# One graph-network kernel on one core: row statistics moved to ScalarE, narrower one-hot windows, merged VectorE instructions

## The chip, the core and the metric

The kernel runs on one core of one Trainium2 chip. A core has TensorE (PE, matrix products into PSUM), VectorE (DVE), ScalarE (ACT), GpSimd (POOL) and SyncE (SP, which here only issues DMAs). Each engine takes its own instructions in order and waits on semaphores for the others. The metric is the device time of one execution in microseconds (us); lower is better. Before the change it is 123.3 us, the median of three runs (123.14 to 123.56).

## The reference

The input is x, 625 nodes by 256 features, 10,625 edges (src, dst; sorted by dst) and one weight for each edge.

```
edge_conv(h, W, b):  m = concat(h[dst], h[src]-h[dst]) @ W + b;  s = segment_sum(m, dst);  return s / max(count, 1)
h = relu(layernorm(x));  xs = [h]
for W, b in three layers:  h = relu(edge_conv(h, W, b));  xs.append(h)
x = x + concat(xs) @ Wf + bf
h = relu(layernorm(x)) @ W4
agg = segment_sum(edge_weight * h[src], dst) + b4;  h = batchnorm over nodes (gamma, beta)
out = x + relu(h)
```

## The kernel before

Gathers and segment sums are done as products with two dense 625 x 625 matrices: `counts` (how many edges run from node s to node d) and the matrix of edge weights (`parts`, the weight split into three bf16 parts so that no accuracy is lost). They are built first, from about 4 to 49 us, and the three layers, the head and the last convolution follow as plain matrix products.

**The build.** The 10,625 edges are 85 tiles of 125 edges. For each tile t one engine makes `src_hot`, a one-hot row of all node numbers for each edge's source (125 x 628, bf16): VectorE with one comparison (`source_tile`, L537), or, for the tiles named in `SCALAR_TILES`, ScalarE with two activations (`distance`, then `src_hot`, L864 and L867). Before the change ScalarE makes tiles 0, 4, 9, 13 early and 38, 57, 76 later. As dst is sorted, a tile's destinations lie in a window of 28 nodes (`WINDOW`). `dst_hot` holds for each block of 17 tiles the one-hot window (`plain_window`, L525) and its products with the three weight parts (`weighted_window`, L531, three instructions). TensorE multiplies the two (L1168, `place`) and adds into five PSUM banks, one for each source block s, four kinds side by side. It goes through five destination blocks r; the list `window_pieces(r)` says which tiles touch block r and with how many nodes (19 or 21 pieces each), so block r costs 5 x 19 or 5 x 21 matmuls with 4 x width columns. For r = 0 the five banks advance tile by tile; for later r bank after bank. ScalarE copies each finished bank out (`copy_block`: `counts`, `parts`). `src_hot` is a ring of 36 tiles; tile t may be written when the blocks that read tile t-36 are done.

**Between the tiles.** Into VectorE's sequence of tiles other work is put at fixed tile numbers: the row statistics of x at tile 8 (`STATS_AT`, five L483 and five L489), reciprocal and shift at tile 11 (`SHIFT_AT`), the vectors and a ones matrix at 19, the low parts of the five neighbour terms u at `U_AT` (L549), the weight differences W_top - W_bottom at `DIFF_AT` (L544), the check of the window's fit at 40 and 74. ScalarE computes the square root (L852), then h0 = relu(norm(x)) in five rows (L898); TensorE transposes them between the pieces of block 0 (L1058), ScalarE copies them back (`h_t`), and after block 0 TensorE computes the neighbour terms of layer 0 (L1079, `neighbour_terms_0`), after block 1 the own terms (L1090). From tile 36 on VectorE also waits for blocks.

**After the build.** `sum_counts` (L1142) adds the counts over sources with a ones matrix, 5 matmuls for each of three column groups; VectorE takes reciprocals (`inverse_rows`, L608, L610) and has_edge (L615). GpSimd waits until all of VectorE's source tiles are made (L441), adds weight parts, splits one weight matrix (L435) and masks the own terms (L452). `sums_0` (L1243, L1264) multiplies u with counts, in two halves of columns; `z_step` (L694 scaling, L698 adding the masked own terms), ScalarE's h_hi (L963) and `h_low` (L704) give layer 1's input; TensorE meanwhile does `head_0` (L1100) and then `neighbour_terms(1)`, which waits for the first two h_low before block 0 and for all four before block 2. Each high part is a copy to a reduced-precision type on ScalarE, each low part the remainder on VectorE.

## Time and profile before

| | before |
|---|---|
| time, median of 3 runs | 123.3 us |
| the profiled execution's own time | 123.12 us |
| its span (first to last instruction) | 121.3 us |
| PE busy, share of the span | 105.4 us, 87% |
| DVE busy | 96.2 us, 79% |
| ACT busy | 59.3 us, 49% |
| POOL busy | 27.6 us, 23% |
| chain that ended last, by engine | PE 58%, DVE 30%, ACT 5%, DMA 2% |

The span starts with the first instruction; the 1.8 us between span and time lie outside it. A busy share is an average over stages; which engine sets the pace in a stage is read from the chain that ended last and from the waits. In the rows further down "start us, us" is the start from the span's begin and the duration. Durations of neighbours overlap a little, so the cost of one of many is the distance of two starts.

### The profile page before, as it was taken

The page shows a single profiled execution, that of the slowest core. Times are in us where ns is not written, and L with a number is a line of the kernel's source. Part 1 is how long each engine was busy: PE and PEld are TensorE (multiplying, and loading weights), DVE is VectorE, ACT ScalarE, POOL GpSimd, SP SyncE. Part 2 cuts the span into 40 slices and gives each one's busy share as a digit, 9 for nine tenths or more (in the row PEclk, how much of TensorE's full clock was granted, in tenths as well). Part 3 has the DMA queues.
Part 4 walks back from the last instruction along what each step waited for, and adds up shares of the span by engine and source line. Part 5 has one row for each costly group of instructions (what it writes and reads, how often), then busy time and mean ns, then how long its engine had stood idle before and what let it go on. Part 6 is the DMA issues. An engine that isn't in the chain of part 4 may idle for free.

```text
span 121.3 us, 2679 instructions
## 1 busy us (share of the span) xinstructions
PE 105.4 (87%) x1034; PEld 97.7 (81%) x1034; DVE 96.2 (79%) x273; ACT 59.3 (49%) x140; POOL 27.6 (23%) x38
## 2 busy tenths in 40 slices
PE   0395799979998899999999999999899997999740
PEld 0355588958797799999899999999799997998630
DVE  0699967999999998859996759966799979707970
ACT  2297988833979877602371313450703343313530
POOL 7100000000000019983329920089300000000000
PEclk9999999999999999999999999999999999999995
DMA  2979400000020002300000300000000000000025
GB/s 48 242 193 268 157 0 5 0 5 0 0 95 0 0 5 67 114 5 3 0 0 6 86 0 0 5 0 0 0 5 0 0 0 0 8 0 0 0 66 146
DMA packets 5402, 4.63 MB, mean 38 GB/s; under 512 B 556, under 2 KB 5387, under 8 KB 5387
## 3 DMA queue, kind: packets, MB, share of 16 engines
q1 hardware_dynamic: 4460, 3.68, 11.2%
q10 hardware_dynamic: 926, 0.75, 2.3%
q8 instruction: 10, 0.16, 0.6%
q14 instruction: 6, 0.04, 0.1%
HBM read 3.79 MB, written 0.64 MB: 37 GB/s over the span
## 4 chain that ended last, share of the span: by engine, by line
PE 58%; DVE 30%; ACT 5%; DMA 2%; issue 2%; SPq 0%
PE bank L1264 13%; DVE src_hot L537 12%; PE bank L1019 9%; PE bank L1021 9%; PE bank L1020 9%; PE bank L1168 8%; PE bank L1100 4%; DVE dst_hot L531 3%; DMA edge_rows_i<-in_dst_dram 2%; DVE stats L483 2%; PE bank L1304 2%; ACT h L898 2%; PE bank L1243 2%; DVE raw L544 1%; DVE u_lo L549 1%
## 5 line engine op out<-in xcount | busy, mean ns | idle before, releaser
L1168 PE MATMUL bank<-dst_hot,src_hot 125*128 125x112 bf16 (+4 forms) x505 | 27.0, 209 | 3.2 <-DVE src_hot L537 2.7
L1168 PEld LDWEIGHTS bank<-dst_hot,src_hot 125*128 125x128 bf16 x505 | 25.0, 99 | 5.8 <-DVE src_hot L537 4.3
L537 DVE TENSOR_SCALAR src_hot<-node_id,edge_cols 125x628 bf16<-125x628 f16 x78 | 24.3, 374 | 0.0
L441 POOL TENSOR_TENSOR parts<-parts 125x625 f32<-125x625 f32 x5 | 7.5, 1502 | 50.1 <-DVE src_hot L537 41.4
L1264 PE MATMUL bank<-counts,u_lo 125*128 125x312 f32 (+1 forms) x60 | 16.3, 307 | 0.0
L963 ACT ACTIVATE h_hi<-pre 128x312 fp32r<-128x312 f32 (+1 forms) x12 | 5.6, 466 | 18.4 <-DVE pre L698 18.4
L1264 PE MATMUL bank<-counts,u_hi 125*128 125x312 f32 (+1 forms) x48 | 14.0, 307 | 0.0
L842 ACT ACTIVATE parts<-bank 125x375 f32<-125x375 f32 x25 | 12.3, 493 | 0.0
L1264 PEld LDWEIGHTS bank<-counts,u_lo 125*128 125x128 f32 x60 | 10.9, 189 | 0.0
L842 ACT ACTIVATE counts<-bank 125x125 fp32r<-125x125 f32 x25 | 7.0, 281 | 6.0 <-PE bank L1168 5.8
L1264 PEld LDWEIGHTS bank<-counts,u_hi 125*128 125x128 f32 x48 | 9.1, 189 | 0.0
L549 DVE TENSOR_TENSOR u_lo<-bank,u_hi 125x256 fp32r<-125x256 f32 x15 | 6.1, 420 | 3.4 <-ACT u_hi L842 3.1
L1021 PE MATMUL bank<-wf_lo,h_hi 128*125 128x256 f32 x30 | 8.4, 281 | 0.0
L1019 PE MATMUL bank<-wf_hi,h_hi 128*125 128x256 f32 x30 | 8.4, 281 | 0.0
L1020 PE MATMUL bank<-wf_hi,h_lo 128*125 128x256 f32 x30 | 8.4, 281 | 0.0
L842 ACT ACTIVATE u_hi<-bank 125x256 fp32r<-125x256 f32 x15 | 5.7, 383 | 4.3 <-PE bank L1021 3.9
L694 DVE TENSOR_TENSOR pre<-bank,inv_count 128x312 f32<-128x312 f32 (+1 forms) x12 | 5.7, 477 | 2.4 <-PE bank L1264 2.4
L842 ACT ACTIVATE weights_hi<-bank 125x500 fp32r<-125x500 f32 (+1 forms) x7 | 3.4, 546 | 7.5 <-PE bank L1304 7.5
L698 DVE TENSOR_TENSOR pre<-pre,own 128x312 f32<-128x312 f32 (+1 forms) x12 | 6.3, 524 | 1.0 <-POOL own L452 0.6
L864 ACT ACTIVATE distance<-node_id,edge_cols 125x628 f16<-125x628 f16 x7 | 5.8, 825 | 2.3 <-DVE edge_cols L520 2.2
L1019 PE MATMUL bank<-weights_hi,u_hi 125*128 125x312 f32 (+1 forms) x20 | 6.2, 312 | 0.7 <-DVE u_lo L761 0.7
L704 DVE SCALAR_TENSOR_TENSOR h_lo<-pre,h_hi 128x312 fp32r<-128x312 f32 (+1 forms) x12 | 6.3, 534 | 0.7
...
## 6 DMA issues: line engine op xcount, KB each, us to landing
raw<-in_L_gnn_W_dram SPq DMA_DIRECT2D x3, 512.0 KB, 6.5
...
raw<-in_L_gnn_Wf_dram SPq DMA_DIRECT2D x1, 512.0 KB, 3.7
...
```

The lines of the kernel that those rows point to most:

```text
L441: step.add(pool.tensor_tensor(part[:, :, 1, :], part[:, :, 1, :], part[:, :, 2, :], ALU.add))
L537: dve.tensor_scalar(src_hot[:, t % RING, :], node_id[:, :], edge_cols[:, 0, t:t + 1], None, ALU.is_equal).then_inc(src_hot_vector, 1)
L549: dve.tensor_tensor(u_lo[:, b, :], groups.bank[name][0:BLK, 0:D], u_hi[:, b, :].bitcast(F32), ALU.subtract).then_inc(u_lo_ready, 1)
L698: dve.tensor_tensor(pre_t[:, f, a:e], pre_t[:, f, a:e], own[:, f, a:e], ALU.add).then_inc(z_ready, 1)
L704: dve.scalar_tensor_tensor(out=h_lo[l + 1][:, f, a:e], in0=pre_t[:, f, a:e], scalar=0.0, in1=h_hi[l + 1][:, f, a:e].bitcast(F32), op0=ALU.max,
L842: copy = lambda o, i: nc.scalar.activation(o, i, ACT.Copy)
L864: nc.scalar.activation(distance[:, :], node_id[:, :], ACT.Abs, bias=edge_cols[:, 0, t:t + 1], scale=-1.0).then_inc(distance_ready, 1)
L1019: pe.matmul(o, lh, rh, start=start, stop=False)
L1020: pe.matmul(o, ll, rh, start=False, stop=False)
L1021: return pe.matmul(o, lh, rl, start=False, stop=stop)
L1168: return pe.matmul(built[s][:, :, n0:n0 + n], src_hot[:, t % RING, BLK * s:BLK * s + P], dst_hot[:, c, :, j // 2, c0:c0 + n, j % 2], start ...
L1264: ins = pe.matmul(bank[KF * h + f][:, 0:e - a], u[:, k, P * f:P * (f + 1)], counts[:, k, a:e], start=False, stop=(k == NB - 1 and u is u_l ...
```

## The change

- The mean and variance of x move from VectorE (five statistics and five aggregations at tile 8) to ScalarE: five passes with Identity whose accumulator output gives the row sums, one small scaling, five passes with Square whose accumulator output gives the sums of squares, and the root. VectorE's shift is a product with the negative mean, at tile 12. ScalarE makes no early source tiles; it makes 36, 40, 55, 72 and 76.
- The three parts of the edge weight are copied by ScalarE, with VectorE doing the subtractions in between.
- The windows that TensorE reads are narrowed by `half_width(t)`: 12 nodes at the ends of the list, then 16, 20 and 24, and 28 in the middle. The number of matmuls stays at 505.
- The degree of a node is no longer summed from five blocks: a column of ones in `src_hot` (number 626) makes it an extra row of the last source block, and `sum_counts` reads that row with one matmul (two for the last column group).
- `weighted_window` is one instruction of 1512 elements in place of three of 504. The u terms of layer 0 are handled two blocks at a time. Source tiles are 626 wide.
- The differences of W1 and W2 move behind the tiles on VectorE; GpSimd waits for the first low part after them. The constants' memsets move from GpSimd to VectorE's idle start. In the batch norm at the end the semaphore's numbers go down by one with the removed aggregation.

```
+def half_width(t):
+    p = (t + 0.5) / TILES
+    return min(WINDOW // 2, 2 * round(2.5 + 9 * math.sqrt(p * (1 - p))))
...
-            pool.wait_ge(src_hot_vector, TILES - len(SCALAR_TILES))
+            pool.wait_ge(w_lo_vector, 1)
...
             def weighted_window(c):
                 dve.wait_ge(window_ready, c + 1)
-                for k in range(1, KINDS):
-                    part = weight_parts[:, k - 1, c, :].rearrange("p (a b) -> p a b", b=2)
-                    ins = dve.tensor_tensor(dst_hot[:, c, k], dst_hot[:, c, 0],
-                                            part.unsqueeze(2).to_broadcast([EP, PAIRS, WINDOW, 2]), ALU.mult)
-                ins.then_inc(weighted_windows_ready, 1)
+                shape = [EP, KINDS - 1, PAIRS, WINDOW, 2]
+                part = weight_parts[:, c].rearrange("p k (a b) -> p k a b", b=2).unsqueeze(3).to_broadcast(shape)
+                plain = dst_hot[:, c, 0].unsqueeze(1).to_broadcast(shape)
+                dve.tensor_tensor(dst_hot[:, c, 1:KINDS], plain, part, ALU.mult).then_inc(weighted_windows_ready, 1)
...
-                if t == STATS_AT:
-                    dve.wait_ge(x_loaded, 32)
-                    for b in range(NB):
-                        moments_of(b)
-                    variances(range(NB))
                 if t == SHIFT_AT:
-                    scale_shift(range(NB), norm_ready)
+                    stds[0] += 1
+                    dve.wait_ge(std_ready, stds[0])
+                    step.add(dve.reciprocal(rstd[0:BLK, 0:NB], rstd[0:BLK, 0:NB]))
+                    step.wait()
+                    dve.tensor_tensor(shift[0:BLK, 0:NB], neg_mean[:, :], rstd[0:BLK, 0:NB],
+                                      ALU.mult).then_inc(norm_ready, 1)
...
+            difference(1)
             low_part(HI_WB1, wb[1][1][:, :, :], raw[1][:, KF:2 * KF, :], wb[1][0][:, :, :])
-            low_part(HI_WD1, wd[1][1][:, :, :], raw[1][:, 0:KF, :], wd[1][0][:, :, :])
             inverse_rows(0)
+            low_part(HI_WD1, wd[1][1][:, :, :], raw[1][:, 0:KF, :], wd[1][0][:, :, :])
             inverse_rows(1)
...
             edge_rows_of(1)
+            difference(2)
...
-            act.wait_ge(edge_cols_ready, 1)
-            act.wait_ge(constants_ready, 4)
-            for t in SCALAR_EARLY[:3]:
-                source_tile(t)
...
+            act.wait_ge(x_loaded, 32)
+            act.wait_ge(padding_ready, 1)
+            for b in range(NB):
+                nc.scalar.activation(h0[:, b, :], x_in[:, b, :], ACT.Identity,
+                                     accum_out=row_sums[:, b:b + 1]).then_inc(row_sums_ready, 1)
+            act.wait_ge(row_sums_ready, NB)
+            nc.scalar.activation(neg_mean[:, :], row_sums[:, :], ACT.Copy, scale=-1.0 / D).then_inc(mean_ready, 1)
+            act.wait_ge(mean_ready, 1)
+            for b in range(NB):
+                nc.scalar.activation(h0[:, b, :], x_in[:, b, :], ACT.Square, bias=neg_mean[:, b:b + 1],
+                                     accum_out=row_squares[:, b:b + 1]).then_inc(row_squares_ready, 1)
...
-                for s in blocks:
-                    ins = pe.matmul(o[:, 0:e - a], ones_r[:, :], part[:, s, a:e], start=(s == 0 and part is counts),
-                                    stop=(s == NB - 1 and part is counts), skip_group_check=True)
-                return ins
+                return pe.matmul(o[:, 0:e - a], degree_r[0:rows, :], part[0:rows, NB - 1, a:e], start=opens, stop=closes,
+                                 skip_group_check=True)
```

How this moves the instructions is shown at three places. The first is VectorE from its first source tile on (L537, in the new kernel L573), before:

```order
L537 TENSOR_SCALAR src_hot<-node_id,edge_cols 125x628 [waits edge_cols_ready]
L537 TENSOR_SCALAR src_hot<-node_id,edge_cols 125x628 x5
L483 BN_STATS stats<-x_in 125x6 [waits x_loaded]
L483 BN_STATS stats<-x_in 125x6 x4
L489 BN_AGGR moments<-stats 125x2 [waits vector_steps] x5
L537 TENSOR_SCALAR src_hot<-node_id,edge_cols 125x628 x2
L497 RECIPROCAL rstd<-rstd 125x5 [waits std_ready]
L499 SCALAR_TENSOR_TENSOR shift<-moments,rstd 125x5 [waits vector_steps]
L537 TENSOR_SCALAR src_hot<-node_id,edge_cols 125x628 x3
L525 TENSOR_TENSOR dst_hot<-pair_id,rel 125x504
L531 TENSOR_TENSOR dst_hot<-dst_hot,weight_parts 125x504 [waits window_ready]
L531 TENSOR_TENSOR dst_hot<-dst_hot,weight_parts 125x504 x2
```

and in the new kernel:

```order
L573 TENSOR_SCALAR src_hot<-node_id,edge_cols 125x626 [waits edge_cols_ready]
L573 TENSOR_SCALAR src_hot<-node_id,edge_cols 125x626 x11
L601 RECIPROCAL rstd<-rstd 125x5 [waits std_ready]
L603 TENSOR_TENSOR shift<-neg_mean,rstd 125x5 [waits vector_steps]
L573 TENSOR_SCALAR src_hot<-node_id,edge_cols 125x626 x3
L562 TENSOR_TENSOR dst_hot<-pair_id,rel 125x504
L569 TENSOR_TENSOR dst_hot<-dst_hot,weight_parts 125x1512 [waits window_ready]
```

The statistics are gone, twelve tiles stand before the reciprocal where there were eight (ScalarE made three of the first eleven), and the weighted window is one instruction of 1512 elements.

The second place is ScalarE around the layer norm's root (`rstd`), before, from the third early source tile on:

```order
L864 ACTIVATE distance<-node_id,edge_cols 125x628 [waits src_hot_scalar]
L867 ACTIVATE src_hot<-distance 125x628 [waits distance_ready]
L852 ACTIVATE rstd<-moments,eps 125x5 [waits variance_ready]
L864 ACTIVATE distance<-node_id,edge_cols 125x628 [waits src_hot_scalar]
L867 ACTIVATE src_hot<-distance 125x628 [waits distance_ready]
L898 ACTIVATE h_104<-x_in,shift,rstd 125x256 [waits norm_ready]
L898 ACTIVATE h_104<-x_in,shift,rstd 125x256 x2
```

and in the new kernel, from the copies of the edge weight's parts on:

```order
L883 ACTIVATE row_parts<-weight_rows 85x125 [waits edge_weights_loaded]
L883 ACTIVATE row_parts<-row_rest 85x125 [waits row_rest_ready] x2
L943 ACTIVATE h_108,row_sums<-x_in 125x256 [waits padding_ready,x_loaded]
L943 ACTIVATE h_108,row_sums<-x_in 125x256 x4
L946 ACTIVATE neg_mean<-row_sums 125x5 [waits row_sums_ready]
L949 ACTIVATE h_108,row_squares<-x_in,neg_mean 125x256 [waits mean_ready]
L949 ACTIVATE h_108,row_squares<-x_in,neg_mean 125x256 x4
L953 ACTIVATE rstd<-row_squares,eps 125x5 [waits row_squares_ready]
L957 ACTIVATE h_108<-x_in,shift,rstd 125x256 [waits norm_ready]
L957 ACTIVATE h_108<-x_in,shift,rstd 125x256 x2
L883 ACTIVATE h_t<-bank 128x2x125 [waits filled]
```

Ten passes over x and a small scaling stand ahead of the root, and no source tile between the root and the rows of h0.

The third place is VectorE behind its last source tiles, before:

```order
L589 TENSOR_SCALAR flag<-worst 1x1 [waits vector_steps]
L537 TENSOR_SCALAR src_hot<-node_id,edge_cols 125x628 [waits block_built] x10
L597 TENSOR_TENSOR wb_lo<-raw_89,wb_hi 128x512 [waits w_hi]
L597 TENSOR_TENSOR wd_lo<-raw_89,wd_hi 128x512 [waits w_hi]
L608 TENSOR_SCALAR inv_count<-bank 128x250 [waits filled,weighted_windows_ready,block_built]
L610 RECIPROCAL inv_count<-inv_count 128x250 [waits counts_bounded]
L608 TENSOR_SCALAR inv_count<-bank 128x250 [waits filled]
L610 RECIPROCAL inv_count<-inv_count 128x250 [waits counts_bounded]
```

and in the new kernel (L580 is a weight difference, L636 a low part):

```order
L628 TENSOR_SCALAR flag<-worst 1x1 [waits vector_steps]
L573 TENSOR_SCALAR src_hot<-node_id,edge_cols 125x626 [waits block_built] x10
L580 TENSOR_TENSOR raw_93<-raw_93 128x512 [waits raw_loaded1]
L636 TENSOR_TENSOR wb_lo<-raw_93,wb_hi 128x512 [waits w_hi]
L647 TENSOR_SCALAR inv_count<-bank 128x250 [waits filled,weighted_windows_ready,block_built]
L649 RECIPROCAL inv_count<-inv_count 128x250 [waits counts_bounded]
L636 TENSOR_TENSOR wd_lo<-raw_93,wd_hi 128x512 [waits w_hi]
L647 TENSOR_SCALAR inv_count<-bank 128x250 [waits filled]
L649 RECIPROCAL inv_count<-inv_count 128x250 [waits counts_bounded]
```

One difference was added ahead of the first low part, for which GpSimd now waits, and the second low part moved behind the first reciprocal. A few instructions further, ahead of the first scaling of z (L735), stands the other difference:

```order
L654 TENSOR_SCALAR has_edge<-bank 128x250 [waits block_built]
L654 TENSOR_SCALAR has_edge<-bank 128x250
L580 TENSOR_TENSOR raw_94<-raw_94 128x512 [waits raw_loaded2]
L735 TENSOR_TENSOR pre<-bank,inv_count 128x312 [waits count_rows_ready,filled]
L739 TENSOR_TENSOR pre<-pre,own 128x312 [waits own_masked,z_read]
```

## Rows read from the trace of the kernel before

**Rows 1.** The chain of waits in order of time (start us, us, what)

```profile
39.27 1.18 DVE src_hot L537 x4
40.51 7.61 PE bank L1168 x161
48.11 0.64 PE bank L1142 x5
48.76 0.91 PE bank L1168 x19
```

**Rows 2.** Timeline of VectorE (start us, us, line, operation, [idle before <-releaser])

```profile
7.62 1.84 DVE L537 TENSOR_SCALAR src_hot<-node_id,edge_cols 125x628 bf16<-125x628 f16 x6
9.38 1.72 DVE L483 BATCH_NORM_STATS2 stats<-x_in 125x6 f32<-125x256 f32 x5
...
18.95 0.42 DVE L549 TENSOR_TENSOR u_lo<-bank,u_hi 125x256 fp32r<-125x256 f32 x1 [1.70 <-ACT u_hi L842]
...
31.01 0.41 DVE L525 TENSOR_TENSOR dst_hot<-pair_id,rel 125x504 bf16<-125x504 f16 x1
31.46 1.08 DVE L531 TENSOR_TENSOR dst_hot<-dst_hot,weight_parts 125x504 bf16<-125x504 bf16 x3
32.46 3.60 DVE L537 TENSOR_SCALAR src_hot<-node_id,edge_cols 125x628 bf16<-125x628 f16 x12
35.97 0.68 DVE L544 TENSOR_TENSOR raw<-raw 128x512 f32<-128x512 f32 x1
```

**Rows 3.** DMA queues in the stretch 5.7 to 6.2 us

```profile
q10 hardware_dynamic: 4, 0.00, 1.3%
```

**Rows 4.** DMA issue of W0 at 3.93 us (KB each, us to landing)

```profile
raw<-in_L_gnn_W_dram SPq DMA_DIRECT2D x1, 512.0 KB, 4.0
```

**Rows 5.** Timeline of ScalarE, the layer norm of x

```profile
11.55 0.30 ACT L852 ACTIVATE rstd<-moments,eps 125x5 f32<-125x5 f32 x1 [0.81 <-DVE moments L489]
...
13.22 1.57 ACT L898 ACTIVATE h<-x_in,shift,rstd 125x256 f32<-125x256 f32 x3
```

**Rows 6.** Timeline of TensorE, the first neighbour and own terms

```profile
17.39 4.56 PE L1079 MATMUL bank<-raw,h_t 128*125 128x256 f32 x20
...
28.06 4.46 PE L1090 MATMUL bank<-h_t,raw 128*128 128x312 f32 x16
```

**Rows 7.** Timeline of ScalarE, copies of counts as column blocks are finished

```profile
42.63 0.28 ACT L842 ACTIVATE counts<-bank 125x125 fp32r<-125x125 f32 x1 [0.30 <-PE bank L1168]
...
43.58 0.28 ACT L842 ACTIVATE counts<-bank 125x125 fp32r<-125x125 f32 x1 [0.30 <-PE bank L1168]
...
46.36 0.28 ACT L842 ACTIVATE counts<-bank 125x125 fp32r<-125x125 f32 x1
...
48.15 0.28 ACT L842 ACTIVATE counts<-bank 125x125 fp32r<-125x125 f32 x1 [0.25 <-PE bank L1168]
```

**Rows 8.** Timeline of GpSimd

```profile
45.00 2.28 POOL L441 TENSOR_TENSOR parts<-parts 125x625 f32<-125x625 f32 x1 [41.37 <-DVE src_hot L537]
...
48.62 1.30 POOL L441 TENSOR_TENSOR parts<-parts 125x625 f32<-125x625 f32 x1
...
51.25 1.28 POOL L435 TENSOR_TENSOR wf_lo<-raw,wf_hi 128x512 fp32r<-128x512 f32 x1
52.50 1.54 POOL L452 TENSOR_TENSOR own<-own,has_edge 128x312 f32<-128x312 f32 x2
```

**Rows 9.** Timeline of VectorE around the first layer's end

```profile
46.48 1.72 DVE L610 RECIPROCAL inv_count<-inv_count 128x250 f32<-128x250 f32 x1
...
53.45 0.93 DVE L698 TENSOR_TENSOR pre<-pre,own 128x312 f32<-128x312 f32 x1 [0.58 <-POOL own L452]
...
59.82 1.10 DVE L704 SCALAR_TENSOR_TENSOR h_lo<-pre,h_hi 128x314 fp32r<-128x314 f32 x2
```

**Rows 10.** Timeline of ScalarE, the third copy of layer 1's neighbour terms

```profile
62.57 0.39 ACT L842 ACTIVATE u_hi<-bank 125x256 fp32r<-125x256 f32 x1 [0.32 <-PE bank L1021]
```

**Rows 11.** Busy time by stretch (us, engines with instructions begun, PEclk, DMA share, GB/s)

```profile
10.30:13.90 3.60, 1.56 (x25) 1.14 (x22) 3.53 (x17) 2.76 (x6) 0.00 (x0) 1.00 0.80 255
```

226 lines of the change are left out of this document (136 added, 90 removed).

## The prediction

> **What bounds the kernel now.** I read the chain of waits first. Up to 40.5 us it runs mostly over VectorE's source tiles; the last link is a run of four of them that ends at 39.27 + 1.18 = 40.45. From there it lies on TensorE: 161 one-hot matmuls, five for a count sum, 19 more [rows 1]. So the build has two bounds: VectorE until tile 69 exists (the last tile that destination block 3 reads), TensorE after it. Then VectorE's timeline [rows 2]: twelve source tiles start 3.51 us apart, 0.293 us for one; a window with its three weighted products costs 1.45 (31.01 to 32.46); a difference of 512 fp32 elements 0.60 (0.68 less the overlap of 0.08); the row statistics hold VectorE from 9.38 on for about 2.0 us, five times 0.33 and five times 0.08; and at tile 23 it waits 1.70 us for ScalarE's first copy of u. What the change is worth is the time at which tile 69 is ready, plus what TensorE saves behind it, less what the layers give back.
>
> **The start of h0.** ScalarE now makes the moments. It can begin when x is there. The queue that carries x has four packets left after 5.7 [rows 3]; W0, issued at 3.93 on the same DMA engines, is complete 4.0 later, at 7.9 [rows 4]. I take 6.9, between 6.2 and 7.9. Then come five passes, a scaling, five passes and the root. The trace shows no accumulator output, so I bound a pass. Three rows of h0 have the same 125x256 tile and take 1.57, that is 0.49 from start to start and 0.59 for the last [rows 5]; they read two operands per partition (scale and shift), a pass here at most one, so below 0.49 is possible and 0.40 is my lower end. Above: if the readout follows in series as a small activation of its own, as the root with 0.30 [rows 5], a pass costs 0.79. I take 0.49, the nearest row. Sum: 6.95 + 2.45 + 0.15 (last pass draining, semaphore) + 0.35 (scaling) + 2.45 + 0.15 + 0.30 = 12.8 for the root, where before it ended at 11.85. VectorE starts its tiles at about 7.45 (7.62 less 0.15 from the merged first window), makes twelve in 3.5 and stands at tile 12 from 10.95: an idle time of 1.85 us that did not exist. Shift costs 0.35, so VectorE resumes at 13.15 and h0 starts at 13.25. Before, ScalarE made a source tile between root and h0, which started at 13.22 [rows 5]. So the later root costs the h0 path nothing, since that tile is gone: transposes and the neighbour terms start near 17.35 as now [rows 6]. Each 0.1 us on a pass moves all that follows by 1.0 us.
>
> The Trainium skill ("ScalarE: Activation LUTs", What ACT_TABLE_LOAD costs) gives an activation with one per-partition operand 280 ns + 0.833 ns per element, with 93 ns of overlap, 0.40 for 256 elements; its two-operand case agrees with the row of 0.59. By it, with a free accumulator, the root would come at 11.9 and the whole 0.9 us earlier than in my sum. The same page (Rules for kernel authors) sends plain adds and multiplies to VectorE, not ScalarE, which speaks against this part: 2.0 us on VectorE against about 5.8 here.
>
> **VectorE from 13.15 to tile 69.** Tiles 12 to 69 less the three that ScalarE makes (36, 40, 55) are 55: 16.1 us. Four windows at 1.30: 5.2. The merged product saves two starts; three of them take 1.08 against 3 x 0.333 [rows 2], so a start is worth about 0.08 and the saving 0.15 (nothing at worst). The u terms come in pairs: 0.34 for 256 elements and 0.26 for 256 more (the difference's rate of 1 ns per element), 0.60 + 0.60 + 0.34 = 1.5. The first pair is there when TensorE has done two blocks: before, one block's u was usable at 18.95, 1.56 after the start at 17.39 [rows 2, 6]; four more matmuls of 0.22 and 0.2 for the wider copy give 20.0, while VectorE arrives at 19.35: a wait of 0.6. One difference 0.6, vectors and fit check 0.6 as before. Sum 13.15 + 16.1 + 5.2 + 1.5 + 0.6 + 0.6 + 0.6 = 37.75, against 40.45: 2.7 earlier. The removed statistics, two differences and the 1.1 us of wait make this up, and two more tiles and the new wait take from it.
>
> Can TensorE be there? Neighbour terms end at 21.75; block 1 needs tile 35, ready at 24.8, and ends near 27.0; own terms 4.3 [rows 6]; block 2 five times 0.95; one count matmul; the first bank of block 3. That is 37.2, so it waits 0.6 for VectorE.
>
> **TensorE behind tile 69.** A bank of 21 pieces (1904 columns) takes 0.95 us, one of 19 pieces (1852 columns) (48.15 - 46.36)/2 = 0.895 [rows 7]. The difference is two narrow pieces, 52 columns, so a narrow one costs 0.027 whatever its width, and the rest 0.84 for 1800 columns, 0.467 ns each. The narrowed windows leave 1808 columns in a bank of block 3 (0.91) and 1368 in one of block 4; with the floor of 0.027 that is 0.68. Saved: 4 x 0.04 + 5 x 0.21 = 1.2. The middle count sum falls from five matmuls (0.64, [rows 1]) to one: 0.5. The layer's first sum starts 2.7 + 1.2 + 0.5 = 4.4 earlier, near 45.3 (before 49.67). The third count sum saves 0.3 more. The first one is covered by the wait for tile 69.
>
> **What is given back.** GpSimd begins when the last source tile is made, at 45.00; its first addition takes 2.28 beside VectorE's two-operand subtractions, a later one 1.30; first masked own term in time for 53.45, 8.45 after its start [rows 8, 9]. Now it waits for the first low part: last tile 37.75 + 0.9 + 0.4 (fit flag) + 2.9 = 41.95, difference 0.6, low part 0.6: 43.15. Its row is as long as before (the second low part and the last difference now collide with it instead), so VectorE's first addition is at 51.55. VectorE itself is free by then: two reciprocals of 1.65 [rows 9], low part and difference bring it to 49.4. From that addition to the last h_low it was 60.92 - 53.45 = 7.47 of gapless work [rows 9], now until 59.0. TensorE reaches the third block of layer 1's neighbour terms, which needs it, at 61.65 before (its copy starts at 62.57 [rows 10], less 0.7 for its matmuls and 0.2 for the drain), 0.7 after the last h_low; now it could be there at 56.95 and waits 2.0. So of 4.7 won only 61.65 - 58.95 = 2.7 are kept. GpSimd's chain, lengthened by the added difference and low part ahead of it, is the new bound there. Nothing later changes, and TensorE's work from that point is the same.
>
> The Trainium skill ("GPSIMD Engine Reference", Specifications) says that its SBUF interfaces are shared with VectorE, with contention for instructions that have two SBUF inputs; the 2.28 against 1.30 agrees. By it a part of GpSimd's row could go either way, some 0.5 us.
>
> Sum: span 121.3 - 2.7 = 118.6; the profiled execution's own time 123.12 - 2.7 = 120.4. The median of the runs stands 0.2 above that execution, so it would be 120.6 for a median; I give 120.5.
>
> The memsets moved to VectorE cost nothing, since it waits for the edges until 3.9; ScalarE's weight copies alternate with VectorE before 5.6 and are ahead of x. The 626-element tile is taken at 0.293; the tiles that ScalarE makes later lie in its idle time.
>
> **Rivals.**
> A, the accumulator is dear: a pass takes 0.6 to 0.79. For it: no row shows one, and each pass must deliver a value per partition. At 0.65 the time is 122.1. The forecast's gain of 2.7 is used up at 0.49 + 0.27 = 0.76; at full series, 0.79, the root comes at 15.8 and the time is 123.5. This is the case of the other side. Against it: ten such serial readouts would have to overlap with nothing.
> B, nothing is given back: GpSimd's row is short enough (the differences don't collide, 1.30 for each addition) or its result isn't last; with 1.0 us less on it the time is 119.5, with a cheap pass on top 118.6. For it: only one of the additions was slow.
> C, the granted clock. It is 1.00 in 10.3 to 13.9 though TensorE works only 1.56 of 3.60 us [rows 11]. Now it stands nearly idle from 11.1 to 13.9, with smaller matmuls ahead. At 1.2 GHz the neighbour terms take twice 4.4; if a third of them falls into it, 1.5 us: 122.0. Against it: before, more than half of that stretch was idle too, and it kept 2.4 GHz.
> D, the merged product or the 626-element tile runs at half rate: 0.8 for each of four windows is 3.2, 123.7; the tile would cost far more. Against it: innermost strides and types are the same.
>
> **Chances.** Forecast 0.50; A 0.20 with 0.06 at or beyond 0.76; B 0.17; C 0.09; D 0.04. Other runs of a kernel agree within 0.3%, about 0.4 us, which is what can be told from no change. Faster: forecast, B, most of A and C, 0.86. Same (122.9 to 123.7): 0.06. Slower: 0.08, from the end of A and from D. The range is 118.6 (B with a cheap pass) to 122.4 (a pass of 0.68).
>
> **What would show it.** Distance of two passes on ScalarE: 0.49 right, over 0.76 no gain. VectorE idle ahead of the reciprocal at tile 12: 1.9. h0 starts near 13.3; first u wait 0.6; tile 69 near 37.8. A bank of block 4 takes 0.68. Count sums are single matmuls. First sum of the layer near 45.3. TensorE waits about 2 us in the neighbour terms of layer 1, behind GpSimd's mask and VectorE's h_low. I am wrong if TensorE doesn't wait there, if VectorE doesn't stand at tile 12, or if TensorE's clock falls before 20 us.

## The result

The changed kernel takes 121.72 us (median of 4 runs, 121.37 to 121.97) against 123.43 for the kernel before in the same comparison; the ratio is 0.986 with a 95% interval of 0.9823 to 0.9896. It is faster, by about 1.7 us or 1.4%; forecast were 120.5 us and a range of 118.6 to 122.4. Ratios, here and below, leave out single executions that took over 1.5% longer than the fastest of the same kernel; medians don't. The profiled execution took 121.97 us with a span of 120.0, so the span fell by 1.3 us, about half of the 2.7 forecast. The page of the changed kernel gives the shares of the chain that ended last as

```profile
PE 43%; DVE 30%; ACT 9%; POOL 6%; issue 5%; DMA 4%; ACTq 1%; DVEq 0%; POOLq 0%
```

where it had been PE 58%, DVE 30%, ACT 5%, DMA 2%: TensorE lost 15 points, and ScalarE's passes over x and GpSimd's additions came in.

ScalarE first. x is there at 6.88, as taken (in the profiled executions of the experiments it comes between 6.66 and 7.27, so starts of two traces are comparable to about 0.4 us unless they are counted from h0). From the timeline of ScalarE in the changed kernel (start us, us, what, [idle before <-releaser]):

```profile
6.88 0.42 ACT L943 ACTIVATE h<-x_in 125x256 f32<-125x256 f32 x1 [1.54 <-DMA x_in<-in_x_dram]
7.21 0.19 ACT L943 ACTIVATION_READ_ACCUMULATOR h<-x_in 125x1 f32 x1
7.30 0.40 ACT L943 ACTIVATE h<-x_in 125x256 f32<-125x256 f32 x1
...
11.87 0.30 ACT L953 ACTIVATE rstd<-row_squares,eps 125x5 f32<-125x5 f32 x1
12.62 1.09 ACT L957 ACTIVATE h<-x_in,shift,rstd 125x256 f32<-125x256 f32 x2 [0.46 <-DVE shift L603]
```

The output of the accumulator is an instruction of its own, of 0.19 us; the next pass starts 0.09 to 0.10 after it, while it still runs. The passes for the mean start 0.40 apart, those for the squares 0.49. The root ends at 12.17, not 12.8, and h0 starts at 12.62.

The granted clock of TensorE, by stretch (us; busy us and instructions of PE, PEld, DVE, ACT, POOL; PEclk; DMA share; GB/s):

```profile
10.00:12.00 2.00, 1.39 (x24) 0.96 (x21) 0.90 (x4) 1.97 (x9) 0.00 (x0) 1.00 1.01 331
12.00:14.00 2.00, 0.66 (x4) 0.43 (x5) 1.73 (x7) 1.54 (x4) 0.00 (x0) 1.00 0.43 150
14.00:16.00 2.00, 1.86 (x22) 1.47 (x21) 2.00 (x6) 2.00 (x7) 0.00 (x0) 0.89 0.05 15
16.00:18.00 2.00, 2.00 (x27) 1.95 (x25) 2.00 (x9) 1.03 (x4) 0.00 (x0) 0.50 0.03 8
18.00:20.00 2.00, 2.00 (x8) 1.60 (x8) 0.80 (x3) 0.82 (x3) 0.00 (x0) 0.76 0.00 0
```

Before, the clock stood at 1.00 ([rows 11] show 10.3 to 13.9, the neighbour terms of [rows 6] ran at 2.4 GHz). Now it is at 0.50, that is 1.2 GHz, from about 15.6 to 19.0 us: through the last transposes of h0, the last pieces of block 0 and the first neighbour terms. Ahead of the transposes of h0 TensorE stood idle for 1.89 us in one piece. Before the change its idle time there was in two pieces, 1.33 and 0.71, around 20 matmuls of full width:

```profile
11.84 1.31 PE L1168 MATMUL bank<-dst_hot,src_hot 125*128 125x112 bf16 x20 [1.33 <-DVE src_hot L537]
13.86 0.93 PE L1058 MATMUL bank<-ident,h 125*128 125x125 f32 x4 [0.71 <-ACT h L898]
```

From the timeline of TensorE in the changed kernel:

```profile
13.28 0.93 PE L1122 MATMUL bank<-ident,h 125*128 125x125 f32 x4 [1.89 <-ACT h L957]
...
17.56 5.25 PE L1144 MATMUL bank<-raw,h_t 128*125 128x256 f32 x20
...
37.44 8.78 PE L1231 MATMUL bank<-dst_hot,src_hot 125*128 125x12 bf16 x181
...
47.05 0.53 PE L1305 MATMUL bank<-counts,u_hi 125*128 125x312 f32 x2
...
60.39 0.38 PE L1082 MATMUL bank<-wb_hi,h_hi 128*125 128x256 f32 x1 [1.18 <-DVE h_lo L745]
```

The neighbour terms take 5.25 us, against 4.56 in [rows 6]. Own terms start at 28.07, to 0.01 us where they stood. The first sum of layer 0 starts at 47.05; the matmul that answers to it stood at 49.49 before. In layer 1 TensorE then waits 1.18 for h_low, where it waited for nothing.

From the timeline of VectorE in the changed kernel:

```profile
12.20 0.19 DVE L601 RECIPROCAL rstd<-rstd 125x5 f32<-125x5 f32 x1 [1.30 <-ACT rstd L953]
...
21.01 0.69 DVE L586 TENSOR_TENSOR u_lo<-bank,u_hi 125x512 fp32r<-125x512 f32 x1 [2.22 <-ACT u_hi L883]
...
37.77 2.13 DVE L573 TENSOR_SCALAR src_hot<-node_id,edge_cols 125x626 bf16<-125x626 f16 x7
...
40.78 2.41 DVE L573 TENSOR_SCALAR src_hot<-node_id,edge_cols 125x626 bf16<-125x626 f16 x8
...
46.39 1.31 DVE L636 TENSOR_TENSOR wd_lo<-raw,wd_hi 128x512 fp32r<-128x512 f32 x1
...
50.29 1.75 DVE L580 TENSOR_TENSOR raw<-raw 128x512 f32<-128x512 f32 x1
...
52.87 0.93 DVE L739 TENSOR_TENSOR pre<-pre,own 128x312 f32<-128x312 f32 x1 [0.43 <-POOL own L478]
...
59.23 1.10 DVE L745 SCALAR_TENSOR_TENSOR h_lo<-pre,h_hi 128x314 fp32r<-128x314 f32 x2
```

Against [rows 2, 9]: VectorE waits 1.30 for the root and 2.22 for u; tile 69 is the fourth of the seven tiles from 37.77, ready near 39.0 (before 40.45). The last tile is done at 43.2, the own addition starts at 52.87 (before 53.45), the last h_low ends at 60.33 (before 60.92). Two subtractions that take 0.67 elsewhere take 1.31 and 1.75. The timeline of GpSimd, to hold against [rows 8]:

```profile
44.47 1.30 POOL L467 TENSOR_TENSOR parts<-parts 125x625 f32<-125x625 f32 x1 [41.07 <-DVE wb_lo L636]
45.85 1.30 POOL L469 TENSOR_TENSOR parts<-parts 125x625 f32<-125x625 f32 x1
...
50.21 1.29 POOL L461 TENSOR_TENSOR wf_lo<-raw,wf_hi 128x512 fp32r<-128x512 f32 x1
```

It begins 0.53 us earlier than before, behind the difference and the low part that now stand ahead of it.

### The profile page after: what moved, and what is told of

Its sections match the earlier page's. It is cut to its first block, busy times and chain, and to the rows that moved or that the text cites. A ratio compares the mean times of both kernels' runs of the same rounds, so it can differ in the third digit from the quotient of the medians.

```text
span 120.0 us, 2675 instructions
## 1 busy us (share of the span) xinstructions
PE 104.8 (87%) x1023; PEld 96.4 (80%) x1023; DVE 95.6 (80%) x268; ACT 61.0 (51%) x158; POOL 27.3 (23%) x32
## 4 chain that ended last, share of the span: by engine, by line
PE 43%; DVE 30%; ACT 9%; POOL 6%; issue 5%; DMA 4%; ACTq 1%; DVEq 0%; POOLq 0%
DVE src_hot L573 13%; PE bank L1082 9%; PE bank L1326 9%; PE bank L1084 9%; PE bank L1083 9%; DMA x_in<-in_x_dram 4%; POOL parts L467 3%; POOL parts L469 2%; ACT h L949 2%; PE bank L1144 2%; ACT h L943 2%; ACT h L957 2%; PE bank L1366 2%; DVE pre L739 2%; DVE h_lo L745 1%
## 5 line engine op out<-in xcount | busy, mean ns | idle before, releaser
L1231 PEld LDWEIGHTS bank<-dst_hot,src_hot 125*128 125x128 bf16 x505 | 24.4, 101 | 3.1 <-DVE src_hot L573 2.0
L1231 PE MATMUL bank<-dst_hot,src_hot 125*128 125x112 bf16 (+10 forms) x505 | 26.3, 209 | 0.5
L573 DVE TENSOR_SCALAR src_hot<-node_id,edge_cols 125x626 bf16<-125x626 f16 x80 | 24.4, 378 | 0.0
L467 POOL TENSOR_TENSOR parts<-parts 125x625 f32<-125x625 f32 x5 | 7.0, 1395 | 49.2 <-DVE wb_lo L636 41.1
L883 ACT ACTIVATE parts<-bank 125x375 f32<-125x375 f32 x25 | 12.9, 531 | 0.0
L586 DVE TENSOR_TENSOR u_lo<-bank,u_hi 125x256 fp32r<-125x256 f32 (+1 forms) x13 | 5.7, 462 | 3.5 <-ACT u_hi L883 3.4
L883 ACT ACTIVATE counts<-bank 125x125 fp32r<-125x125 f32 (+1 forms) x25 | 7.8, 313 | 0.9 <-PE bank L1231 0.8
L883 ACT ACTIVATE u_hi<-bank 125x256 fp32r<-125x256 f32 (+1 forms) x13 | 5.3, 417 | 5.0 <-PE bank L1084 3.3
L735 DVE TENSOR_TENSOR pre<-bank,inv_count 128x312 f32<-128x312 f32 (+1 forms) x12 | 5.7, 476 | 1.5 <-PE bank L1326 1.5
L1082 PE MATMUL bank<-wb_hi,h_hi 128*125 128x256 f32 x20 | 5.8, 290 | 1.2 <-DVE h_lo L745 1.2
```

Source lines behind the costliest of these rows:

```text
L467: step.add(pool.tensor_tensor(part[:, :, 1, :], part[:, :, 1, :], part[:, :, 2, :], ALU.add))
L573: dve.tensor_scalar(src_hot[:, t % RING, 0:IDS], node_id[:, 0:IDS], edge_cols[:, 0, t:t + 1], None, ALU.is_equal).then_inc(src_hot_vector, 1)
L586: dve.tensor_tensor(u_lo[:, b:b + n, :], rows, u_hi[:, b:b + n, :].bitcast(F32), ALU.subtract).then_inc(u_lo_ready, n)
L735: dve.tensor_tensor(pre_t[:, f, a:e], groups.bank[("z", l, q)][:, 0:e - a], inv_count[:, a:e], ALU.mult).then_inc(z_read, 1)
L883: copy = lambda o, i: nc.scalar.activation(o, i, ACT.Copy)
L1082: pe.matmul(o, lh, rh, start=start, stop=False)
```

## The experiments

All ratios are to the kernel before, which ran on the same chip in each comparison; what is compared with the changed kernel (0.986, span 120.0) says so. A run is one kernel; its trace is of one execution.

**Run e1_warm: eight matmuls in TensorE's idle stretch.**

```
 def turn_h0(b):
+    o = fill(("h0", b))
+    if b == 0:
+        for _ in range(8):
+            pe.matmul(o[:, :], zeros_bf[:, :], node_id[:, 0:512], start=True, stop=True)
     pe.wait_ge(h0_ready, b + 1)
-    o = fill(("h0", b))
...
```

> The changed kernel with eight matmuls of 512 columns of zeros more, put on TensorE ahead of the first transpose of h0, into the bank that this transpose uses. They fill the stretch from 11.4 us, in which TensorE stands idle until h0 is there at 13.3. Theory 1 (the fall of the granted clock to 0.50 from 15.6 to 19.0 us comes from that idle stretch and costs time on the path): clock 1.00 throughout, neighbour terms 4.5 us (changed kernel: 5.25), VectorE's wait at tile 28 falls from 2.2 to about 1.4, its last source tile, GpSimd's start and the whole come 0.8 earlier: ratio to before about 0.980 (changed kernel 0.986). Theory 2 (the fall costs nothing, since what follows is given back to GpSimd and VectorE anyway): clock 1.00, but the time as the changed kernel's, 0.986. Theory 3 (it is the small matmuls after 13.3, not the idle stretch): the clock falls all the same and the time is 0.986.

121.02 us, ratio 0.9831 (0.9807 to 0.9855), span 119.3. A stretch of this kernel, columns as above:

```profile
16.00:18.00 2.00, 1.86 (x31) 1.64 (x29) 2.00 (x10) 1.39 (x6) 0.00 (x0) 1.00 0.00 0
```

Its neighbour terms, on TensorE's timeline:

```profile
17.49 4.56 PE L1147 MATMUL bank<-raw,h_t 128*125 128x256 f32 x20
```

And the first difference of u, on VectorE's:

```profile
20.25 0.69 DVE L586 TENSOR_TENSOR u_lo<-bank,u_hi 125x512 fp32r<-125x512 f32 x1 [1.07 <-ACT u_hi L883]
```

The clock stays at 1.00, the neighbour terms are back at 4.56, u_lo starts 0.76 earlier, and the span falls by 0.7. The first theory holds, with 0.7 where it said 0.8. In this execution x came 0.39 later (h0 starts at 13.01 for 12.62). Counted from the start of h0, u_lo comes 7.24 behind it where it was 8.39: so the fall cost 1.15 us there, 0.46 ahead of the neighbour terms and 0.69 in them. By time the gain is 0.7 us between the medians and 0.4 by the ratios, whose intervals (0.9831 and 0.986) overlap; so it rests on these starts, on the next run, and on the mean granted clock of the four executions of each kernel: 0.973 to 0.977 in the changed one, 0.989 to 0.993 here.

**Run e3_full: all windows 28 nodes wide** (`half_width` returns `WINDOW // 2`), with nothing put into TensorE's idle stretch.

> The changed kernel with all windows at their full width of 28 columns (half width 14 for every tile); TensorE then has 52 more columns in a bank of block 3 and 432 in one of block 4, and as many in blocks 0 and 1. Theory 1 (TensorE's saved columns are given back: it waits for VectorE's h_low in layer 1 anyway): first sum of the layer 1.2 us later than in the changed kernel (48.2), TensorE's idle time in the neighbour terms of layer 1 smaller by the same, the whole at most 0.3 later: ratio 0.986 to 0.988. Theory 2 (TensorE bounds the end of the build and what it saves stays): 1.2 us later, ratio 0.996. On the clock: if the narrowed early windows made it fall, it is 1.00 here from 13 to 20 us and neighbour terms take 4.5; if the idle stretch did, it falls as before.

121.06 us, ratio 0.9829 (0.9806 to 0.9851), span 119.3. The same stretch of this kernel:

```profile
16.00:18.00 2.00, 1.83 (x31) 1.66 (x29) 2.00 (x10) 1.34 (x6) 0.00 (x0) 1.00 0.03 8
```

Its timeline of TensorE, the 181 pieces of blocks 3 and 4 and the third block of layer 1:

```profile
36.71 9.27 PE L1231 MATMUL bank<-dst_hot,src_hot 125*128 125x12 bf16 x181
...
59.67 0.38 PE L1082 MATMUL bank<-wb_hi,h_hi 128*125 128x256 f32 x1 [0.79 <-DVE h_lo L745]
```

Three results. The clock stays at 1.00 although TensorE is idle ahead of h0 here too. But that idle time is 1.22 us now and not 1.89, since the wider matmuls last longer; so this run changes both the width and the idle time, and which of the two the fall hangs on is not separated.

Second, the narrowed windows save less than they seem to. Read bank by bank from the starts of the matmuls, a bank of block 4 takes 0.90 with full windows and 0.77 narrowed, but a bank of block 3 takes 0.95 full and 0.97 narrowed. In blocks 3 and 4 matmuls of 112 columns start 51 to 52 ns apart (medians), those of 96 columns 55, those of 80 columns 37: from 112 to 96 columns nothing is saved. Behind tile 69 the narrowed windows save 0.6 us in all.

Third, the 0.6 us more of matmuls cost nothing at the end. The first sum is at 46.91, even 0.14 earlier than in the changed kernel, and TensorE still waits 0.79 for h_low. So in the changed kernel the narrowed windows as a whole did harm: 0.4 us by the ratios and 0.7 by the medians, through the clock, and no gain that reaches the end.

**Run e4_stats: the statistics back on VectorE**, windows narrow. `SCALAR_EARLY` is (0, 4, 9, 13) again, five statistics and aggregates stand ahead of tile 8, and the shift ahead of tile 11.

> The changed kernel with the row statistics of x back on VectorE (five statistics and five aggregates ahead of tile 8, shift at tile 11) and tiles 0, 4, 9 and 13 back on ScalarE; all the rest as changed. Theory 1 (the move of the statistics bought VectorE nothing here: 2.05 us of work and 1.17 of tiles on ScalarE stand against four more tiles, an idle 1.30 at tile 12 and the fallen clock): h0 starts 0.6 later, near 13.2, but the clock stays at 1.00, the first pair of u is there at 20.0, VectorE waits about 1.2 for it at tile 28, and all behind it is 0.7 to 1.0 earlier than in the changed kernel: ratio to before about 0.980. Theory 2 (taking the statistics from VectorE is what made the kernel faster): last source tile 1.3 to 2.0 us later than in the changed kernel, ratio 0.997 to 1.0.

122.22 us, ratio 0.9931 (0.9905 to 0.9957), span 121.1. Neither theory foresaw this. Stretches of this kernel:

```profile
12.00:14.00 2.00, 1.11 (x21) 0.79 (x19) 1.93 (x8) 1.97 (x4) 0.00 (x0) 0.75 0.73 256
...
18.00:20.00 2.00, 2.00 (x20) 1.74 (x19) 0.58 (x2) 1.53 (x5) 0.00 (x0) 0.54 0.00 0
```

And the first difference of u on VectorE's timeline:

```profile
22.05 0.69 DVE L587 TENSOR_TENSOR u_lo<-bank,u_hi 125x512 fp32r<-125x512 f32 x1 [3.47 <-ACT u_hi L884]
```

The clock falls earlier and for longer (0.50 from 13.0 to 19.8 us), and VectorE waits 3.47 us for u. This run can't price the statistics. The next one can.

**Run e8_stats_full: statistics on VectorE, windows full.**

> The changed kernel with the row statistics back on VectorE and four source tiles back on ScalarE, and with all windows 28 columns wide, so that the granted clock does not fall. To be held against the run with full windows and the statistics on ScalarE (span 119.3, ratio 0.983). Theory 1 (the move of the statistics is worth next to nothing, since VectorE then waits 1.3 to 1.5 for the root and 1.1 for u): clock 1.00 from 13 to 20 us, h0 0.3 later, u_lo at 20.55 after a wait of about 2 us, span 119.6, ratio 0.985. Theory 2 (the move is the source of the gain): ratio 0.993 or more. Rival on the clock (the stretch without statistics passes is itself the cause): the clock falls here too, ratio 0.993.

121.04 us, ratio 0.9828 (0.9811 to 0.9844). With the clock at 1.00 in both, moving the statistics changes nothing: 0.9828 here, 0.9829 in e3_full. The spans, 118.8 and 119.3, say little: x came late in the execution of e3_full (h0 at 12.99), and e10_gate_full below, which is e3_full up to the last tile but had x at 6.84, has that tile within 0.02 us of this run's. The first theory holds, though u was there sooner than it said (19.88, not 20.55). What VectorE saved it spent waiting, 1.5 us for the root and 1.1 for u, against 1.64 for u here.

**Run e2_later: the shift ahead of tile 16**, transposes behind tiles 15, 16 and 17.

```
-SHIFT_AT, VECS_AT, DIFF_AT = 12, 20, 37
+SHIFT_AT, VECS_AT, DIFF_AT = 16, 20, 37
...
-jobs = {12: (0, 1), 14: (2, 3), 16: (4,)}
+jobs = {16: (0, 1), 17: (2, 3), 18: (4,)}
```

> The changed kernel with VectorE's shift ahead of tile 16 instead of 12, and TensorE's transposes of h0 behind tiles 15, 16 and 17 instead of 11, 13 and 15, so that both make and use tiles while ScalarE takes the statistics. Theory 1: VectorE's idle 1.30 at tile 12 goes, TensorE works until 12.4 and its clock stays 1.00, so u comes 0.7 earlier; but VectorE is at tile 28 1.2 earlier, so the idle time moves there (2.2 - 0.7 + 1.2 = 2.7 us), and the last tile and the whole gain only the clock's 0.7: ratio about 0.980. Theory 2 (VectorE is bound by its own work, the idle time at tile 12 was the loss): last tile 1.3 to 2.0 earlier, ratio 0.972. Theory 3: the clock falls anyway, ratio 0.986.

123.13 us, ratio 1.0 (0.9979 to 1.0022): the whole gain is gone. I had overlooked that the next block's windows stand ahead of tile 15, and so ahead of the shift. VectorE's timeline of this kernel:

```profile
13.61 0.18 DVE L601 RECIPROCAL rstd<-rstd 125x5 f32<-125x5 f32 x1
```

And ScalarE's, the first rows of h0:

```profile
14.02 1.59 ACT L957 ACTIVATE h<-x_in,shift,rstd 125x256 f32<-125x256 f32 x3 [1.83 <-DVE shift L603]
```

The root is there at 12.2, but its reciprocal comes at 13.61, and h0 starts 1.4 later than in the changed kernel (14.02 for 12.62). The span is 1.3 longer (121.3 for 120.0), but not because h0 is late. TensorE had used more tiles by then, so less stood between the transposes, and the neighbour terms start where they did:

```profile
17.58 6.22 PE L1144 MATMUL bank<-raw,h_t 128*125 128x256 f32 x20
```

A stretch of this kernel shows what happened then:

```profile
18.00:20.00 2.00, 2.00 (x6) 1.52 (x6) 0.44 (x2) 1.11 (x5) 0.00 (x0) 0.50 0.04 8
```

The clock falls here too, 2.0 us later than in the changed kernel: it is at 0.50 from 17.5 to 21.0 us, and nearly all of that lies on the neighbour terms. They take 6.22 for 5.25, u_lo starts at 22.01 for 21.01, and the 1.0 us stands at every later point up to the last matmuls (the third block of layer 1 is at 61.37 for 60.39). The other 0.3 comes at the very end, where the clock falls again before the last matmuls are done. So of the three theories the third has the clock right and the time wrong, since I had not asked what the fall would cover.

**Run e9_noacc: the ten passes without the accumulator output** (mean and variance are then not computed).

> The changed kernel with ScalarE's ten passes over x kept, but without the accumulator output (the sums are constants, so mean and variance are not computed). Theory 1 (the accumulator read of 0.19 us overlaps the next pass and costs nothing from start to start): passes still 0.40 apart for the mean and 0.49 for the squares, root within 0.2 us of the changed kernel's 11.87 (only the last read before each dependent step, 0.1 each, goes). Theory 2 (it costs 0.09 a pass): squares 0.40 apart, root 0.6 to 0.7 earlier.

One execution, 120.06 us and a span of 118.3. The timeline of ScalarE:

```profile
6.83 1.64 ACT L945 ACTIVATE h<-x_in 125x256 f32<-125x256 f32 x5 [0.92 <-DMA x_in<-in_x_dram]
...
8.75 2.10 ACT L950 ACTIVATE h<-x_in,neg_mean 125x256 f32<-125x256 f32 x5
```

Five passes for the mean take 1.64 and five for the squares 2.10, so they are 0.31 and 0.40 apart. The accumulator costs 0.09 us a pass, 0.9 in all; the root starts 0.98 earlier, at 10.89. The second theory holds, with 0.98 for its 0.6 to 0.7, since the passes for the mean lose the 0.09 as well. By the Trainium skill ("ScalarE: Activation LUTs", What ACT_TABLE_LOAD costs) a pass with one operand per partition takes 280 ns + 0.833 ns per element, of which 93 ns overlap the pass before; for 256 elements that is an estimate of 0.40. This run agrees, and with the accumulator it is 0.49. The clock stayed at 1.00 in this run too, with h0 0.8 us earlier; both together make the 1.7 us by which the span is shorter than the changed kernel's. Held against e1_warm, whose clock also stayed at 1.00 and whose windows are as narrow, this run shows what a shift of h0 is worth: h0 starts 1.21 earlier (11.80 for 13.01), u_lo 1.14 (19.11 for 20.25), the own addition 1.13 (50.96 for 52.09), and the span is 1.0 shorter. With ScalarE's passes at the front, nearly all of it reaches the end, as the forecast had it ("each 0.1 us on a pass moves all that follows by 1.0 us").

**Runs e6_diff2, e7_mask, e7_both: what binds the place at which the gain is given back.** e6_diff2 moves VectorE's last difference behind the last h_low (and ScalarE's copy of it behind the copies of h). e7_mask moves one low part on GpSimd:

```
-low_part(HI_WF1, ...)
 mask_own_0(0)
 ...
 mask_own_0(1)
+low_part(HI_WF1, ...)
```

e7_both does both.

> The changed kernel with VectorE's last weight difference (raw[2]) moved from ahead of the first masked sum of layer 0 to behind its last h_low, and ScalarE's copy that needs it behind its four copies of h. In the changed kernel this difference takes 1.75 us beside GpSimd's additions, and VectorE then waits 0.43 for GpSimd's masked own term. Theory 1 (GpSimd's row of additions is the bound of that place, as I had predicted): VectorE is at its first product near 50.3 instead of 52.0 and waits about 1.6 for GpSimd; the last h_low 0.1 to 0.4 earlier: ratio 0.983 to 0.986. Theory 2 (VectorE's own work is the bound): last h_low 1.6 earlier, ratio 0.974.

> The changed kernel with one step of GpSimd moved: the low part of Wf for layer 1 (1.29 us at 50.21) comes behind the masked own terms of layer 0 instead of ahead of them, so that the first masked own term is there about 1.25 us earlier, near 51.2. VectorE's own row stays. Theory 1 (GpSimd is the bound): the gain ends where VectorE's row takes over: its own addition starts at 52.4 instead of 52.9, ratio 0.982. Theory 2 (VectorE's collisions decide all): 0.986 as the changed kernel.

> Both moves of the last two together. Theory 1 (two rows, GpSimd's and VectorE's, end 0.43 us apart at the same place, so that either move alone gains nearly nothing): own addition near 51.2, last h_low 1.5 to 1.7 earlier, TensorE's wait of 1.2 us plus 1.4 of late weight loads in layer 1 goes, span 1.2 to 1.5 below the changed kernel's: ratio 0.974 to 0.976. Theory 2 (the moved steps are in somebody's way later, or TensorE stands behind something else there): ratio 0.983 or more.

121.71, 121.44 and 121.35 us; ratios 0.988 (0.9842 to 0.9918), 0.9838 (0.9803 to 0.9874) and 0.9807 (0.9769 to 0.9845). The clock falls in the profiled executions of all three, and their times scatter by over 1%, so the traces are read from the end of VectorE's last tile, which is the start of its next difference. VectorE in e6_diff2, that difference and the own addition:

```profile
43.15 0.67 DVE L580 TENSOR_TENSOR raw<-raw 128x512 f32<-128x512 f32 x1
...
52.44 0.93 DVE L738 TENSOR_TENSOR pre<-pre,own 128x312 f32<-128x312 f32 x1 [1.65 <-POOL own L478]
```

VectorE in e7_mask, with the last difference between them:

```profile
42.97 0.67 DVE L580 TENSOR_TENSOR raw<-raw 128x512 f32<-128x512 f32 x1
...
50.15 0.68 DVE L580 TENSOR_TENSOR raw<-raw 128x512 f32<-128x512 f32 x1
...
51.65 0.93 DVE L739 TENSOR_TENSOR pre<-pre,own 128x312 f32<-128x312 f32 x1 [0.43 <-POOL own L478]
```

VectorE in e7_both:

```profile
43.22 0.67 DVE L580 TENSOR_TENSOR raw<-raw 128x512 f32<-128x512 f32 x1
...
51.52 0.93 DVE L738 TENSOR_TENSOR pre<-pre,own 128x312 f32<-128x312 f32 x1 [0.65 <-POOL own L478]
```

The own addition starts 9.75 us after the last tile in the changed kernel (52.87 - 43.12), 9.29 in e6_diff2, 8.68 in e7_mask and 8.30 in e7_both. For e6_diff2 the first theory holds: VectorE is ready 1.65 us earlier and waits 1.65 instead of 0.43 for GpSimd. For e7_mask I had expected 0.43 and it is 1.07, because the difference at 50.15 now takes 0.68 and not 1.75: GpSimd stands between two instructions there and waits 0.20 for has_edge, until 50.31. The two rows are coupled. In e7_both less than expected arrives: an addition at 57.48 takes 1.05 instead of 0.49, beside the low part that I had moved there, and TensorE still waits 0.44. Its third block of layer 1 comes 16.39 after VectorE's last tile, against 17.27 in the changed kernel: 0.88 gained of the 1.45. By time none of the three can be told from the changed kernel: the intervals overlap.

**Run e10_gate_full: GpSimd let go at VectorE's last tile**, with full windows: its wait is for `src_hot_vector` again, and not for `w_lo_vector`.

> The changed kernel with full windows (clock 1.00; that run had ratio 0.983, GpSimd's start 43.76, VectorE's own addition 52.15, last h_low ending 59.6), and GpSimd's additions let go as soon as VectorE's last source tile is made, not behind the next difference and low part. Theory 1 (GpSimd's row, started late by those two, is what binds the own addition): GpSimd starts 1.2 earlier, near 42.5, the wait of 0.43 goes, last h_low 0.4 earlier, ratio 0.980. Theory 2 (VectorE's additions and subtractions of two operands stand still until GpSimd's running instruction ends): the difference and the low part stretch from 0.67 to up to 1.9 each, VectorE's row is 0.6 to 1.5 later, ratio 0.988 or more.

120.82 us, ratio 0.9806 (0.9782 to 0.9829); e3_full has 0.9829 (0.9806 to 0.9851). The number is the first theory's, but the two can't be told apart by time, and its reason fails. Most of the difference between the two traces is no effect of the edit: x came 0.41 us earlier here, and the last tile is 0.44 earlier (e3_full's difference starts at 42.40, this kernel's at 41.97). Counted from the last tile, GpSimd starts 1.2 us earlier and the own addition comes after 9.5 us instead of 9.75, which is 0.2 gained. The traces show why so little comes of it. GpSimd in this kernel:

```profile
42.13 2.29 POOL L467 TENSOR_TENSOR parts<-parts 125x625 f32<-125x625 f32 x1 [38.73 <-DVE src_hot L573]
44.49 1.30 POOL L469 TENSOR_TENSOR parts<-parts 125x625 f32<-125x625 f32 x1
```

And VectorE:

```profile
42.57 0.67 DVE L636 TENSOR_TENSOR wb_lo<-raw,wb_hi 128x512 fp32r<-128x512 f32 x1
...
45.24 1.10 DVE L636 TENSOR_TENSOR wd_lo<-raw,wd_hi 128x512 fp32r<-128x512 f32 x1
```

It is GpSimd that stands here: its addition takes 2.29 and ends 1.2 us after VectorE's two subtractions are through (44.42 and 43.24). The second theory had the sides wrong: VectorE had started first and kept going. VectorE's second subtraction even went ahead although GpSimd's addition had been started 0.44 earlier. The own addition is then at 51.51, after the same wait of 0.43.

**Runs e11_best_act and e12_best_dve: all that was learned, with the statistics on either engine.** Common edits: full windows for the first 19 tiles, `U_AT` (33, 34, 36), and the two moves of e7_both. e11_best_act has the statistics on ScalarE, the shift ahead of tile 15 (before the windows this time) and the transposes at `jobs = {15: (0, 1), 16: (2, 3), 17: (4,)}`; e12_best_dve has the statistics on VectorE and the transposes as the changed kernel.

> Five edits on the changed kernel, statistics still on ScalarE: windows of the first 19 tiles at full width (clock), shift ahead of tile 15 (last tile before the next windows) with TensorE's transposes of h0 behind tiles 14 to 16, the u differences at tiles 33, 34 and 36, low part of Wf behind GpSimd's masked terms, last difference behind the last h_low. Theory 1 (VectorE's waits of 1.3 at the root and 1.1 at u, and the pair of rows at the masked terms, are all that keeps TensorE waiting): clock 1.00, both waits under 0.5, last tile 1.5 or more earlier than with full windows alone, TensorE's wait in layer 1 gone, span 117.3 to 118.0, ratio 0.968 to 0.974. Theory 2 (TensorE bounds already and these waits cover each other): ratio 0.978 or more.

> As the last, but with the statistics on VectorE, four early source tiles on ScalarE and the transposes where the changed kernel has them. Where VectorE no longer waits for u, its 2.0 us of statistics count. Theory 1: VectorE's time at tile 33 is about the same in both (2.05 of statistics against five tiles' worth of idle time and tiles that ScalarE makes), so the two are within 0.3%: ratio 0.968 to 0.974. Theory 2 (moving statistics off VectorE pays once VectorE's other waits are gone): this one is 0.7 us or more slower than the run with ScalarE's statistics.

118.13 us, ratio 0.9587 (0.9558 to 0.9615), span 116.2, and 119.14 us, ratio 0.9669 (0.9642 to 0.9695), span 117.4. TensorE in e11_best_act:

```profile
16.44 4.56 PE L1147 MATMUL bank<-raw,h_t 128*125 128x256 f32 x20
...
35.03 8.26 PE L1234 MATMUL bank<-dst_hot,src_hot 125*128 125x12 bf16 x181
...
44.40 0.52 PE L1308 MATMUL bank<-counts,u_hi 125*128 125x312 f32 x2
```

And in e12_best_dve:

```profile
17.71 4.56 PE L1139 MATMUL bank<-raw,h_t 128*125 128x256 f32 x20
...
45.67 0.52 PE L1300 MATMUL bank<-counts,u_hi 125*128 125x312 f32 x2
```

Both are faster than I expected, and e11_best_act beats both kernels: 3.6 us below the changed one. It has no wait of VectorE for u at all, 0.55 for the root, and none of TensorE's matmuls waits between 17 and 66 us. Its first sum comes 2.65 before the changed kernel's (47.05 - 44.40). Of this 1.12 is the earlier start of the neighbour terms (17.56 to 16.44: 0.46 of it by the clock, as e1_warm shows, the rest because tiles 12 to 14 were used while h0 was being made and less stands between the transposes), 0.69 the clock (neighbour terms), 0.60 block 1, whose 105 pieces no longer wait for tiles, and 0.24 the waits among the 181 pieces less a later start of the sum. The other 1.15 us of the span is the wait in layer 1. The difference between the two kernels is there when the neighbour terms start (1.27 us) and is 1.27 still at the first sum; 0.77 of it is the first transpose of h0 (13.41 and 14.18), the rest the place of the transposes. But most of the 0.77 is when the inputs came: in e12_best_dve's execution VectorE's first source tile starts at 7.88, in e11_best_act's at 7.30, and with the statistics on VectorE h0 follows that tile by 5.66 us (e4_stats, e8_stats_full and e12_best_dve alike). That accounts for 0.58 and leaves 0.2. What is measured is the pair: 1.0 us between the medians, with intervals apart. How much of it is the statistics and how much the place of the transposes, which were moved in one of the two only, was not run by itself.

## Why the forecast was right in kind and too large in size

**The start of h0: right in mechanism, 0.6 too late.** I took 0.49 for every pass. That is right for the squares (0.49) and too much for the mean (0.40), which reads no operand per partition; without the accumulator, they are 0.40 and 0.31. Root at 12.17 for 12.8, VectorE's new idle time 1.30 for 1.85, h0 at 12.62 for 13.25. Rival A (an accumulator dear enough to eat the gain) is refuted: it costs 0.09 a pass.

**The step that failed: "transposes and the neighbour terms start near 17.35 as now", at the same speed.** This is the loss that rival C names, to which I gave 0.09. The neighbour terms did start at 17.56, but only because h0 was 0.6 early, and they ran in part at 1.2 GHz. "Before, more than half of that stretch was idle too, and it kept 2.4 GHz" was no protection: TensorE is busy 2.05 of the 4 us from 10 to 14 now, as the windows show, and by [rows 11] it had been busy 1.56 of 3.60; what had changed is how wide its matmuls are and how its idle time lies, and e1_warm and e3_full don't separate these. VectorE's wait for u became 2.22 instead of 0.6, the pair ready at 21.01 instead of 20.0. From the start of h0 to u I had 6.75 us; it took 8.39, and 7.24 and 7.30 in e1_warm and e3_full, where the clock stayed up. So the fall cost 1.15, where rival C had 1.5, and 0.4 to 0.7 by time. The other 0.5 lies mostly between h0 and the neighbour terms, 4.5 in both runs for my 4.1; e11_best_act, which had used more tiles by then, needs 3.7.

**VectorE to tile 69:** 39.0 for 37.75. The late u makes 1.0 of the 1.25; windows with the merged product took 1.31 (1.30 forecast). Rival D is refuted with that.

**TensorE behind tile 69: the wait right, the saving twice too large.** Its wait was put at 0.6; the 181 pieces take 8.78 where 8.26 is their time in e11_best_act, so 0.5 or a little more. The term of 1.2 for the narrowed windows is mis-sized: they save 0.6. I had priced every column at 0.467 ns above a floor; a bank of block 4 takes 0.77 and not 0.68, and one of block 3 is 0.02 slower than the full one, not 0.04 faster. The middle count sum costs 0.20 instead of 0.13. The first sum was put at 45.3 and came at 47.05: it is 2.4 earlier than before, not 4.4. (I had counted 45.3 from the chain's 49.67; the timeline has that sum at 49.49, which makes it 45.1.) Of the 2.0 that are missing, tile 69 makes 1.3 and the windows 0.6.

**Given back: right in its form, shifted by the same 1.3.** GpSimd's first addition to the own addition took 8.40 (forecast 51.55 - 43.15 = 8.40), from there to the end of the last h_low 7.46 (forecast 7.45). But it all started 1.3 us late, because VectorE's last tile did. So TensorE won 2.4 by the first sum, 2.5 by the start of layer 1's neighbour terms (57.56 for 60.06), and kept 1.3; the forecast was 4.4, 4.7 and 2.7. "GpSimd's chain is the new bound there" is only half right. GpSimd's row and VectorE's end 0.43 us apart, and each holds the other up. I had put this down as "its row is as long as before" without asking what VectorE's subtractions beside it would take: I had VectorE ready 2.15 us ahead of the own addition, and it was 0.43.

**The chances.** The time lies in the range and nearest to rival C's 122.0, at a place where forecast and rival C both happened. That the range held it is in part luck: its upper end stood for a dear accumulator, which did not happen, and losses that I had put at nothing or too small (the clock, the width of the windows) filled that room, while a cheaper accumulator gave 0.6 back. By the prediction's own list one sign of being wrong came true, TensorE's clock fell before 20 us, and a bank of block 4 took 0.77 for 0.68. Rival B (nothing given back) is refuted by TensorE's 1.18 us of waiting.
